# Attention scores from two full and two half-height products a tile, two tiles at a time

## The chip, the cores and the metric

The kernel runs on one core of one Trainium2 chip. The metric is the time of one execution in microseconds of device time, as a median over runs. TensorE is called PE here, VectorE DVE, ScalarE ACT, GpSimd POOL, and SyncE SP.

## The reference

`x` has the shape 4 x 1024 x 128 (batch, positions, features). Two layers follow each other, each of the form x = x + s * silu(ffn(norm(x))). The change lies in the attention of the first layer:

```python
qkv = (x @ qkv_w.T).reshape(B, S, 3, H, D)        # H = 16 heads, D = 64
q, k = rope(q), rope(k)
scores = einsum('bhqd,bhkd->bhqk', q, k) * SCALE
kb = -p * log1p(a * abs(pos_k - pos_q))           # p, a: one number a head
attn = softmax(scores + kb, axis=-1)
out = einsum('bhqk,bhkd->bhqd', attn, v)
s = out.reshape(B, S, H * D) @ out_w.T
```

There are 4 x 16 pairs of a batch and a head, each with 1024 x 1024 scores. The first layer's second part is a mixture of eight experts, the second layer a recurrence over time and a feed-forward part with low-rank additions.

## The kernel before

The program runs six blocks one after the other: `prepare`, `experts`, `project`, `attend`, `recur` and `finish`. Each block has one instruction stream for each engine, and the streams meet at semaphores. The order of the work in each stream is written out by hand.

**Numbers in two parts.** The attention works on pairs of bf16 numbers: a value is rounded to bf16 (the high part), and what the rounding left is kept as a second bf16 number (the low part). A product of two such values is put together from products of parts that are added up in PSUM.

**`project`** (lines 743 to 901) makes q and k for two heads at a time. There are 64 jobs: 8 pairs of heads, 4 batches, 2 pieces of 512 positions. In a job PE does four fp32 products of 512 columns (L900); DVE multiplies by sine and cosine and adds (L783, L784, L788) and leaves q and k of both heads in `rq`, with one head in partitions 0 to 63 and the other in 64 to 127. ACT rounds them into the high parts (`hi_part`, L796), and POOL subtracts to get the low parts (`lo_part`, L802). `parts` holds for each partition the four pieces q high, q low, k high, k low, of 512 numbers each. ACT's queue then writes all four with one DMA (`write`, L807) into the DRAM tensor `qk_parts`, whose order is (batch and pair of heads, partition, piece, position). Each of four buffers of `parts` has a semaphore `qk_wr`, which the rounding waits for before it writes the buffer again.

**Loads of scores' operands.** `load_scores_in` (L904 to L913) is called by SP for each head. It fills three tiles of 128 partitions and 1024 columns: `QS` holds q high in the upper 64 partitions and q low in the lower 64, `KS` holds k high twice and `KL` holds k low twice. Each half of a tile is one DMA of 64 rows of 2 KB, so there are six. The tiles exist twice, one set for each head of a pair.

**`attend`** (lines 923 to 1273) works on tiles of 128 queries of one head and one batch: 8 tiles are a half (`BT`), the two halves of a pair of heads are one turn of the loop (`U` = 16 tiles), and there are 32 turns (`NI`), 512 tiles in all. The turns go over the 4 batches of a pair of heads before the next pair comes. The work is a software pipeline: `step(it, u)` on each engine handles different tiles at different lags. `LV` = 2 belongs to the product with v, `LT` = 11 to the turn, `LE` = 12 to the exponent and `LS` = 13 to the scores.

- PE, `scores` (L1059): for each half of 512 keys, the product QS x KS (L1068) and QS x KL (L1069) are added in PSUM, four products of 128 rows a tile. There are two score tiles `score_ps`; before it writes one, PE waits for `biased`, which says that DVE has read the tile two before.
- DVE, `bias_max` (L1143): adds the bias table to the scores, writes them to SBUF and takes the row maximum.
- ACT, `exp` (L1224): exponents and row sums. POOL, `low` (L1256): low part of the exponents.
- PE, `turn` (L1077): eight transposes of 128 columns of the high part into `turn_ps`. ACT (L1231) or DVE (L1158) copies them out, four tiles of a half each. The low part is transposed by a DMA that SP issues (L1016).
- PE, `by_v`: in steps 0 to 3 of a half four products of 128 rows and 512 columns with the high parts (L1096), in steps 4 and 5 eight products that use 64 columns of the array each, in pairs, with the low parts (L1101).
- In step 6 DVE and ACT take the result out in two parts (`take_out`, L1163, L1166, L1236); in step 7 PE multiplies it by the output weights (`out`, 24 products of 128 columns, L1113 to L1115). DVE scales and POOL adds the shares (L1175, L1185, L1264).

In each of its steps PE does: scores, turn, `out` if it is due, `by_v` if it is due. DVE does: `take_out` if due, `bias_max`, `add_share` or `invert` if due, `scale_share` if due, copy of a turned tile if it is DVE's.

SP's stream (`units`, L1018) issues for each tile the transposing DMA, once a half the load of v, after the tiles in `LOADS` the loads for the next turn's scores, and at the tiles in `PIECES` a quarter of the bias table of the next pair of heads (only around the last batch of a pair).

Of the kernel before, what the change touches and what calls it, by code (L numbers as in the profile page):

```python
# [20 lines left out]
P = 128  # L21
# [721 lines left out]
def project(nc, K, io, sb, ps, sem):  # L743
# [46 lines left out]
    def hi_part(act, gi, j):  # L790

        s = j % 4
        act.wait_ge(pair, gi * NJ + (j + 3))

        act.wait_ge(qk_wr[s], gi * (DMA * NJ // 4) + (DMA * (j // 4) + 1))
        act.copy(parts[s][:, 0::2, :], rq[s][:]).then_inc(hi_ready, 1)  # L796

    def lo_part(g, gi, j):

        s = j % 4  # L800
        g.wait_ge(hi_ready, gi * NJ + (j + 1))
        g.tensor_tensor(parts[s][:, 1::2, :], rq[s][:], parts[s][:, 0::2, :], ALU.subtract).then_inc(lo_ready, 1)  # L802

    def write(act, gi, j):
        b, c, s = j // NC, j % NC, j % 4
        act.wait_ge(lo_ready, gi * NJ + (j + 2 + LEAD))
        act.dma_start(K.qkscr[bass.ds(gi + b * G, 1), :, :, c * CH:c * CH + CH].rearrange("o p k c -> (o p) k c"),  # L807
                      parts[s][:]).then_inc(qk_wr[s], DMA)

    with nc.Block() as block:  # L810

        @block.sync
        def _(sp):
            with sp.Fori(0, G // 2 - 1) as gh:
                for r in range(2):

                    sp.wait_ge(qk_ready, gh * (2 * NJ) + (r + 1) * NJ)
                    sp.dma_start(wqk[r][:], io["wqk"][bass.ds(gh * 2 + (r + 2), 1)].rearrange("o p k m -> (o p) k m")).then_inc(wqk_in[r], DMA)

            for s in range(4):  # L820
                sp.wait_ge(qk_wr[s], DMA * NJ // 4 + 1)

            for s in range(2):
                load_scores_in(sp, K, 0, s)
                for k in range(4):
                    load_table(sp, K, 0, s, k)
# [77 lines left out]
def load_scores_in(sp, K, ix, s):  # L904

    q = K.qkscr[bass.ds(ix % B * G + ix // B, 1)].rearrange("o p k c -> (o p) k c")
    rows = slice(s * DH, s * DH + DH)
    sp.dma_start(K.QS[s][0:DH, :], q[rows, 0, :]).then_inc(K.qk_in[s], DMA)
    sp.dma_start(K.QS[s][DH:P, :], q[rows, 1, :]).then_inc(K.qk_in[s], DMA)
    sp.dma_start(K.KS[s][0:DH, :], q[rows, 2, :]).then_inc(K.qk_in[s], DMA)  # L910
    sp.dma_start(K.KS[s][DH:P, :], q[rows, 2, :]).then_inc(K.qk_in[s], DMA)
    sp.dma_start(K.KL[s][0:DH, :], q[rows, 3, :]).then_inc(K.qk_in[s], DMA)
    sp.dma_start(K.KL[s][DH:P, :], q[rows, 3, :]).then_inc(K.qk_in[s], DMA)  # L913

# [8 lines left out]
def attend(nc, K, io, sb, ps, sem):  # L923
# [18 lines left out]
    WB, ident16 = K.WB, K.ident16  # L942
    QS, KS, KL, TB = K.QS, K.KS, K.KL, K.TB
    VV = [sb(f"v_hi_lo{s}", [P, BT, 2 * DH], BF16) for s in range(2)]
# [31 lines left out]
    LV = 2  # L976
    LS, LE, LT = LV + 11, LV + 10, LV + 9
    HI_STEPS, V_STEPS, OUT_STEP, PROJ_STEP = 4, 6, 6, 7
# [15 lines left out]
    with nc.Block() as block:  # L994

        LOADS = (BT, U - 1)
        PIECES = {BT - 2: [(0, 0)], BT - 1: [(0, 1)], BT + 1: [(0, 2)], BT + 2: [(0, 3)],
                  U - 2: [(1, 0)], U - 1: [(1, 1)], 0: [(1, 2)], 1: [(1, 3)]}

        @block.sync  # L1000
        def _(sp):
# [40 lines left out]
            for s in range(4):  # L1042
                sp.wait_ge(K.qk_wr[s], G * (DMA * S * B // CH // 4) + 1)
            for b in range(B):
# [12 lines left out]
        @block.tensor  # L1057
        def _(pe):
            def scores(it, n):  # L1059
                s, t, k = n // BT % 2, n % BT, n // U  # L1060
                if t == 0:
                    pe.wait_ge(qk_in[s], at(it, 6 * DMA, 6 * DMA * (k + 1)))
                if not (isinstance(it, int) and it == 0 and n < 2):
                    pe.wait_ge(biased, at(it, U, n - 1))
                o, q = sp_[n % 2], slice(t * P, t * P + P)
                cs = [slice(c * CH, c * CH + CH) for c in range(2)]
                for c in range(2):
                    pe.matmul(o[:, cs[c]], QS[s][:, q], KS[s][:, cs[c]], start=True, stop=False)  # L1068
                    mm = pe.matmul(o[:, cs[c]], QS[s][:, q], KL[s][:, cs[c]], start=False, stop=True)  # L1069
                mm.then_inc(s_ready, 1)  # L1070

# [46 lines left out]
            def step(it, u, there):  # L1118
                n = u + LV
                if there(u + LS):  # L1120
                    scores(it, u + LS)
                if there(u + LT):
                    turn(it, u + LT)
                if there(n) and n % BT == PROJ_STEP:
                    out(it, n // BT)
# [567 lines left out]
def program(nc, io):  # L1693

    with ExitStack() as outer:
# [18 lines left out]
        K.vscr = nc.dram_tensor("v_parts", [NT, P, H, 2 * DH], BF16, kind="Internal").ap()  # L1714
        K.qkscr = nc.dram_tensor("qk_parts", [B * G, P, 4, S], BF16, kind="Internal").ap()

# [9 lines left out]
        with ExitStack() as heads:  # L1726
            sb_in, _ = maker(heads)
            home = [K.X[:, 4 * i:4 * i + 4, :].rearrange("p t d -> p (t d)").bitcast(BF16) for i in range(6)]
            K.QS, K.KS, K.KL = [home[2 * i:2 * i + 2] for i in range(3)]
            K.TB = [sb_in(f"bias_tab{s}", [P, TAB]) for s in range(2)]  # L1730
# [79 lines left out]
```

## Time and profile before

| What | Value |
|---|---|
| median of 3 runs | 1956.33 us |
| lowest, highest | 1954.63, 1957.67 us |
| the profiled execution's own time | 1963.61 us |
| its span | 1961.8 us |
| mean granted clock of PE | 0.97 of full speed |
| PE busy | 1816.5 us |
| DVE busy | 1505.1 us |
| POOL busy | 1406.9 us |
| ACT busy | 1151.3 us |
| the queue that carries SP's and ACT's transfers | 682272 packets, 245.23 MB |
| DMA transfers of `qk_parts` into the score operands | 384 of 128 KB |

The span runs from the first to the last instruction on the core. The profiled execution took 1.8 us more than its span and 7.3 us more than the median of the runs. An engine's busy time is the sum of the stretches in which it worked. The duration of a PE product in a record contains its way through the array, so that consecutive products overlap in the records; the distance from one start to the next is what a product costs in a row of products. In a timeline, one row can stand for several instructions of the same group (x8), and its start is that of the first.

### The profile page before, as it was taken

To read this page: it belongs to the slowest core of one execution; us is meant where nothing else is said; L and a number is where in the kernel's file an instruction comes from. 1 tells how busy PE (TensorE), PEld (TensorE's weight loads), DVE (VectorE), ACT (ScalarE), POOL (GpSimd) and SP (SyncE) were. 2 spreads that over 40 slices of the span, in tenths; PEclk is the share of its full clock that TensorE was granted. 3 is DMA by queue.
4 is the path that set the end of the run, shared out by engine and by line. 5 is a ranking of instruction groups with operands and counts; after the bars stand their busy time and mean duration, and the time that the engine had idled before them with its cause. 6 is when DMAs were issued, how large, how long until landed. Compare 5 with 4: busy or idle time off the path is not lost. (4 is left out here: it accounts for less than half of the span.)

```text
span 1961.8 us, 40038 instructions
## 1 busy us (share of the span) xinstructions
PE 1816.5 (93%) x12356; PEld 1042.4 (53%) x12356; DVE 1505.1 (77%) x3016; ACT 1151.3 (59%) x1727; POOL 1406.9 (72%) x811
## 2 busy tenths in 40 slices
PE   4959989999799999999999999999999999799888
PEld 2625653333355555555555555555555555356656
DVE  5224559999788889789888888888788888688841
ACT  5525332222577777677777777777777777412133
POOL 5260217888699899799899899799899899555421
PEclk8979989999899999999999999999999999889989
DMA  4233515556488988988988988988988988500001
GB/s 153 87 106 150 159 40 168 160 169 217 148 169 189 205 184 178 191 185 179 199 187 180 192 188 181 189 187 182 188 185 181 206 189 174 129 0 1 1 6 38
DMA packets 721637, 295.28 MB, mean 151 GB/s; under 512 B 620096, under 2 KB 687682, under 8 KB 721552
## 3 DMA queue, kind: packets, MB, share of 16 engines
q1 hardware_dynamic: 682272, 245.23, 58.0%
q10 hardware_dynamic: 37248, 46.14, 6.6%
q0 software_dynamic: 2048, 3.15, 0.6%
q8 instruction: 23, 0.38, 0.1%
q14 instruction: 46, 0.38, 0.1%
HBM read 102.39 MB, written 58.85 MB: 82 GB/s over the span
## 5 line engine op out<-in xcount | busy, mean ns | idle before, releaser
L1256 POOL TENSOR_TENSOR probs_lo<-probs 128x1024 bf16<-128x1024 f32 x512 | 959.0, 1893 | 125.1 <-ACT probs L1224 68.9
L1143 DVE CUSTOM_DVE_ANT_0 scores<-score_ps,bias_tab 128x1024 f32<-128x1024 f32 x512 | 620.9, 1221 | 119.8 <-issue 117.5
L1224 ACT ACTIVATE probs<-scores,neg_max 128x1024 f32<-128x1024 f32 x512 | 587.6, 1148 | 192.7 <-DVE neg_max L1143 191.6
L1068 PE MATMUL score_ps<-x 128*128 128x512 bf16 x1024 | 391.5, 382 | 23.2 <-DVE neg_max L1143 12.0
L1069 PE MATMUL score_ps<-x 128*128 128x512 bf16 x1024 | 389.9, 381 | 0.0
L1077 PEld LDWEIGHTS turn_ps<-ident_bf,probs 128*128 128x128 bf16 x4096 | 266.7, 98 | 145.6 <-ACT probs L1224 34.3
L1077 PE MATMUL turn_ps<-ident_bf,probs 128*128 128x128 bf16 x4096 | 313.7, 220 | 9.7 <-ACT probs L1224 7.3
L1096 PE MATMUL pv_ps<-probs_t_hi,v_hi_lo 128*128 128x512 bf16 x1024 | 262.7, 379 | 0.3 <-DVE share L1175 0.3
L1231 ACT COPY probs_t_hi<-turn_ps 128x1024 bf16<-128x1024 bf16 x256 | 254.9, 996 | 2.9
L900 PE MATMUL proj_ps<-xn_t,wqk 128*128 128x512 f32 x512 | 232.7, 608 | 7.9 <-DVE rotated L788 4.0
L802 POOL TENSOR_TENSOR qk_parts<-rotated,qk_parts 128x1024 bf16<-128x1024 f32 x64 | 136.1, 2127 | 110.1 <-ACT qk_parts L796 108.8
L1068 PEld LDWEIGHTS score_ps<-x 128*128 128x128 bf16 x1024 | 100.1, 98 | 170.4 <-DVE neg_max L1143 52.3
L1158 DVE COPY probs_t_hi<-turn_ps 128x1024 bf16<-128x1024 bf16 x256 | 172.8, 675 | 0.1
L796 ACT CAST qk_parts<-rotated 128x1024 bf16<-128x1024 f32 x64 | 66.9, 1045 | 179.6 <-DVE rotated L788 143.2
L900 PEld LDWEIGHTS proj_ps<-xn_t,wqk 128*128 128x128 f32 x512 | 92.7, 191 | 147.3 <-issue 103.6
L1069 PEld LDWEIGHTS score_ps<-x 128*128 128x128 bf16 x1024 | 100.6, 98 | 91.2 <-issue 1.4
L1101 PE MATMUL pv_ps<-probs_t_lo,v_hi_lo 128*64 128x512 bf16 x1024 | 134.7, 385 | 0.0
L1460 POOL TENSOR_TENSOR q_state<-state,q_t 128x1024 f32<-128x1024 f32 x32 | 76.1, 2379 | 78.8 <-DVE state L1406 71.6
L1096 PEld LDWEIGHTS pv_ps<-probs_t_hi,v_hi_lo 128*128 128x128 bf16 x1024 | 87.1, 98 | 62.7 <-issue 0.4
L1224 ACT ACTIVATION_READ_ACCUMULATOR probs<-scores,neg_max 128x1 f32 x512 | 96.6, 189 | 0.0
L1113 PE MATMUL pv_ps<-wo_parts,out_t_hi 128*128 (+1 forms) x512 | 91.2, 221 | 2.3 <-DVE out_t_lo L1166 2.3
L1114 PE MATMUL pv_ps<-wo_parts,out_t_hi 128*128 (+1 forms) x512 | 90.5, 221 | 0.0
(228 smaller groups left out, 2404.6 us busy)
## 6 DMA issues: line engine op xcount, KB each, us to landing
x<-qk_parts SPq DMA_DIRECT2D x384, 128.0 KB, 2.9
qk_parts<-qk_parts ACTq DMA_DIRECT2D x64, 512.0 KB
v_hi_lo<-v_parts SPq DMA_DIRECT2D x64, 256.0 KB, 3.2
bias_tab<-bias_by_distance SPq DMA_DIRECT2D x64, 240.0 KB, 3.6
probs_t_lo<-probs_lo SPq DMA_TRANSPOSE x512, 3.3
v_parts<-cos_tables ACTq DMA_DIRECT2D x12, 512.0 KB
v_parts<-sin_tables ACTq DMA_DIRECT2D x12, 512.0 KB
xn<-in_x SPq DMA_DIRECT2D x4, 512.0 KB, 5.7
```

What stands on the lines that cost most here:

```text
L802: g.tensor_tensor(parts[s][:, 1::2, :], rq[s][:], parts[s][:, 0::2, :], ALU.subtract).then_inc(lo_ready, 1)
L900: mm = pe.matmul(pp[s][:, i, :], wqk[r][:, i, :], rows, start=True, stop=True)
L1068: pe.matmul(o[:, cs[c]], QS[s][:, q], KS[s][:, cs[c]], start=True, stop=False)
L1069: mm = pe.matmul(o[:, cs[c]], QS[s][:, q], KL[s][:, cs[c]], start=False, stop=True)
L1077: mm = pe.transpose(tp[n % 2][:, k, :], PRB[n % NP][:, k * P:k * P + P], ident16[:])
L1096: mm = pe.matmul(ov[i][:], VV[h][:, k, :], PT[:, r:r + 4, k, :], start=(k == 0), stop=False, skip_group_check=True)
L1101: mm = pe.matmul(ov[c][c * DH:c * DH + DH], VV[h][:, k, 0:DH], LO[:, r:r + 4, k, :], start=False, stop=(k == BT - 1), skip_group_check=True)
L1143: v.tensor_tensor_reduce(SB[n % 2][:], sp_[n % 2][:], TB[s][:, j:j + S], -1.0, 3.0e38, ALU.add, ALU.min, neg_max[:, n % 16:n % 16 + 1]).th ...
L1158: v.tensor_copy(PT[:, n % U, :, :], tp[n % 2][:]).then_inc(hi_dve, 1)
L1224: act.activation(PR[n % NP][:], SB[n % 2][:], ACT.Exp, bias=neg_max[:, m:m + 1], scale=-1.0, accum_out=row_sum[:, m:m + 1]).then_inc(exped, 1)
L1231: act.copy(PT[:, n % U, :, :], tp[n % 2][:]).then_inc(hi_act, 1)
L1256: g.tensor_tensor(LQ[n % NL][:], PR[n % NP][:], PRB[n % NP], ALU.subtract).then_inc(low_made, 1)
```

## The change

Three things change.

**The parts.** `parts` now holds q low, q high, k high, k low in this order. `qk_parts` in DRAM is ordered by (batch and pair of heads, head, piece, row of the head, position). A job is written by two DMAs of 64 partitions each, so the counts of `qk_wr` double.

**The loads.** With this order three loads of 128 rows of 2 KB fill a head's tiles: `QB` has q low above q high, `QK` has q high above k high, `KK` has k high above k low. `LOADS` moves from tiles 8 and 15 to tiles 6 and 14, and four entries of `PIECES` move forward by one tile.

**The scores.** For each half of 512 keys, a full product QB x KK gives q low x k high + q high x k low, and a product of 64 rows adds q high x k high. That product takes partitions 0 to 63 of QK and KK for the first 512 keys, and partitions 64 to 127 of QB and QK for the second 512. The product of the two low parts, which the kernel before added, is left out. In every second step PE does the full products of a tile, a turn, the full products of the next tile, and then the four half-height products of both tiles (`high_parts`); in the other steps it does a turn alone. `LS` becomes 14 and `LE` 13.

```diff
--- before.py
+++ after.py
@@ -792,20 +792,21 @@
         s = j % 4
         act.wait_ge(pair, gi * NJ + (j + 3))
 
-        act.wait_ge(qk_wr[s], gi * (DMA * NJ // 4) + (DMA * (j // 4) + 1))
-        act.copy(parts[s][:, 0::2, :], rq[s][:]).then_inc(hi_ready, 1)
+        act.wait_ge(qk_wr[s], gi * (2 * DMA * NJ // 4) + (2 * DMA * (j // 4) + 1))
+        act.copy(parts[s][:, 1:3, :], rq[s][:]).then_inc(hi_ready, 1)
 
     def lo_part(g, gi, j):
 
         s = j % 4
         g.wait_ge(hi_ready, gi * NJ + (j + 1))
-        g.tensor_tensor(parts[s][:, 1::2, :], rq[s][:], parts[s][:, 0::2, :], ALU.subtract).then_inc(lo_ready, 1)
+        g.tensor_tensor(parts[s][:, 0::3, :], rq[s][:], parts[s][:, 1:3, :], ALU.subtract).then_inc(lo_ready, 1)
 
     def write(act, gi, j):
         b, c, s = j // NC, j % NC, j % 4
         act.wait_ge(lo_ready, gi * NJ + (j + 2 + LEAD))
-        act.dma_start(K.qkscr[bass.ds(gi + b * G, 1), :, :, c * CH:c * CH + CH].rearrange("o p k c -> (o p) k c"),
-                      parts[s][:]).then_inc(qk_wr[s], DMA)
+        for h in range(2):
+            rows = K.qkscr[bass.ds(gi + b * G, 1), h, :, :, c * CH:c * CH + CH].rearrange("o k p c -> (o p) k c")
+            act.dma_start(rows, parts[s][h * DH:h * DH + DH]).then_inc(qk_wr[s], DMA)
 
     with nc.Block() as block:
 
@@ -818,7 +819,7 @@
                     sp.dma_start(wqk[r][:], io["wqk"][bass.ds(gh * 2 + (r + 2), 1)].rearrange("o p k m -> (o p) k m")).then_inc(wqk_in[r], DMA)
 
             for s in range(4):
-                sp.wait_ge(qk_wr[s], DMA * NJ // 4 + 1)
+                sp.wait_ge(qk_wr[s], 2 * DMA * NJ // 4 + 1)
 
             for s in range(2):
                 load_scores_in(sp, K, 0, s)
@@ -903,14 +904,9 @@
 
 def load_scores_in(sp, K, ix, s):
 
-    q = K.qkscr[bass.ds(ix % B * G + ix // B, 1)].rearrange("o p k c -> (o p) k c")
-    rows = slice(s * DH, s * DH + DH)
-    sp.dma_start(K.QS[s][0:DH, :], q[rows, 0, :]).then_inc(K.qk_in[s], DMA)
-    sp.dma_start(K.QS[s][DH:P, :], q[rows, 1, :]).then_inc(K.qk_in[s], DMA)
-    sp.dma_start(K.KS[s][0:DH, :], q[rows, 2, :]).then_inc(K.qk_in[s], DMA)
-    sp.dma_start(K.KS[s][DH:P, :], q[rows, 2, :]).then_inc(K.qk_in[s], DMA)
-    sp.dma_start(K.KL[s][0:DH, :], q[rows, 3, :]).then_inc(K.qk_in[s], DMA)
-    sp.dma_start(K.KL[s][DH:P, :], q[rows, 3, :]).then_inc(K.qk_in[s], DMA)
+    rows = K.qkscr[bass.ds(ix % B * G + ix // B, 1), s].rearrange("o k p c -> (o k p) c")
+    for i, dst in enumerate((K.QB, K.QK, K.KK)):
+        sp.dma_start(dst[s], rows[i * DH:i * DH + P, :]).then_inc(K.qk_in[s], DMA)
 
 
 def load_table(sp, K, g, s, k):
@@ -940,7 +936,7 @@
     recip = sem("recip")
 
     WB, ident16 = K.WB, K.ident16
-    QS, KS, KL, TB = K.QS, K.KS, K.KL, K.TB
+    QB, QK, KK, TB = K.QB, K.QK, K.KK, K.TB
     VV = [sb(f"v_hi_lo{s}", [P, BT, 2 * DH], BF16) for s in range(2)]
     SB = [sb(f"scores{i}", [P, S]) for i in range(2)]
     NP, NL = 4, 4
@@ -974,7 +970,7 @@
     NI = B * G
     U = 2 * BT
     LV = 2
-    LS, LE, LT = LV + 11, LV + 10, LV + 9
+    LS, LE, LT = LV + 12, LV + 11, LV + 9
     HI_STEPS, V_STEPS, OUT_STEP, PROJ_STEP = 4, 6, 6, 7
 
     def run(eng, step):
@@ -993,9 +989,9 @@
 
     with nc.Block() as block:
 
-        LOADS = (BT, U - 1)
-        PIECES = {BT - 2: [(0, 0)], BT - 1: [(0, 1)], BT + 1: [(0, 2)], BT + 2: [(0, 3)],
-                  U - 2: [(1, 0)], U - 1: [(1, 1)], 0: [(1, 2)], 1: [(1, 3)]}
+        LOADS = (BT - 2, U - 2)
+        PIECES = {BT - 3: [(0, 0)], BT - 1: [(0, 1)], BT: [(0, 2)], BT + 1: [(0, 3)],
+                  U - 3: [(1, 0)], U - 1: [(1, 1)], 0: [(1, 2)], 1: [(1, 3)]}
 
         @block.sync
         def _(sp):
@@ -1040,7 +1036,7 @@
             for s in range(2):
                 load_v(0, s)
             for s in range(4):
-                sp.wait_ge(K.qk_wr[s], G * (DMA * S * B // CH // 4) + 1)
+                sp.wait_ge(K.qk_wr[s], G * (2 * DMA * S * B // CH // 4) + 1)
             for b in range(B):
                 units(0, b)
             with sp.Fori(1, G - 1) as g:
@@ -1056,18 +1052,26 @@
 
         @block.tensor
         def _(pe):
+            halves = [slice(c * CH, c * CH + CH) for c in range(2)]
+
             def scores(it, n):
-                s, t, k = n // BT % 2, n % BT, n // U
-                if t == 0:
-                    pe.wait_ge(qk_in[s], at(it, 6 * DMA, 6 * DMA * (k + 1)))
+                s, k = n // BT % 2, n // U
+                if n % BT == 0:
+                    pe.wait_ge(qk_in[s], at(it, 3 * DMA, 3 * DMA * (k + 1)))
                 if not (isinstance(it, int) and it == 0 and n < 2):
                     pe.wait_ge(biased, at(it, U, n - 1))
-                o, q = sp_[n % 2], slice(t * P, t * P + P)
-                cs = [slice(c * CH, c * CH + CH) for c in range(2)]
-                for c in range(2):
-                    pe.matmul(o[:, cs[c]], QS[s][:, q], KS[s][:, cs[c]], start=True, stop=False)
-                    mm = pe.matmul(o[:, cs[c]], QS[s][:, q], KL[s][:, cs[c]], start=False, stop=True)
-                mm.then_inc(s_ready, 1)
+                q = slice(n % BT * P, n % BT * P + P)
+                for cs in halves:
+                    pe.matmul(sp_[n % 2][:, cs], QB[s][:, q], KK[s][:, cs], start=True, stop=False)
+
+            def high_parts(n):
+                s = n // BT % 2
+                for i in range(2):
+                    q = slice((n + i) % BT * P, (n + i) % BT * P + P)
+                    for c, cs in enumerate(halves):
+                        rows = slice(c * DH, c * DH + DH)
+                        mm = pe.matmul(sp_[i][:, cs], (QK, QB)[c][s][rows, q], (KK, QK)[c][s][rows, cs], start=False, stop=True)
+                    mm.then_inc(s_ready, 1)
 
             def turn(it, n):
                 pe.wait_ge(exped, at(it, U, n + 1))
@@ -1117,10 +1121,14 @@
 
             def step(it, u, there):
                 n = u + LV
-                if there(u + LS):
+                pair = there(u + LS) and (u + LS) % 2 == 0
+                if pair:
                     scores(it, u + LS)
                 if there(u + LT):
                     turn(it, u + LT)
+                if pair:
+                    scores(it, u + LS + 1)
+                    high_parts(u + LS)
                 if there(n) and n % BT == PROJ_STEP:
                     out(it, n // BT)
                 if there(n) and n % BT < V_STEPS:
@@ -1712,7 +1720,7 @@
         K.eout = nc.dram_tensor("expert_rows", [E * CAP, D], F32, kind="Internal").ap()
         K.fscr = nc.dram_tensor("bias_by_distance", [H, FLEN], F32, kind="Internal").ap()
         K.vscr = nc.dram_tensor("v_parts", [NT, P, H, 2 * DH], BF16, kind="Internal").ap()
-        K.qkscr = nc.dram_tensor("qk_parts", [B * G, P, 4, S], BF16, kind="Internal").ap()
+        K.qkscr = nc.dram_tensor("qk_parts", [B * G, 2, 4, DH, S], BF16, kind="Internal").ap()
 
         def run(block):
             with ExitStack() as own:
@@ -1726,7 +1734,7 @@
         with ExitStack() as heads:
             sb_in, _ = maker(heads)
             home = [K.X[:, 4 * i:4 * i + 4, :].rearrange("p t d -> p (t d)").bitcast(BF16) for i in range(6)]
-            K.QS, K.KS, K.KL = [home[2 * i:2 * i + 2] for i in range(3)]
+            K.QB, K.QK, K.KK = [home[2 * i:2 * i + 2] for i in range(3)]
             K.TB = [sb_in(f"bias_tab{s}", [P, TAB]) for s in range(2)]
             K.WB, K.ident16 = sb_in("wo_parts", [P, 2, H, P], BF16), sb_in("ident_bf16", [P, P], BF16)
             with ExitStack() as layer0:
```

## Rows read from the trace of the kernel before

**Rows 1.** The page, busy us, share of the span and count of instructions.

```profile
PE 1816.5 (93%) x12356; PEld 1042.4 (53%) x12356; DVE 1505.1 (77%) x3016; ACT 1151.3 (59%) x1727; POOL 1406.9 (72%) x811
```

**Rows 2.** Busy time by stretch: its length, engines' busy us, PEclk, DMA share, GB/s.

```profile
core 0: us, PE busy (x) PEld busy (x) DVE busy (x) ACT busy (x) POOL busy (x), PEclk, DMA share, GB/s
...
526.00:1686.00 1160.00, 1135.85 (x9698) 658.44 (x9698) 992.04 (x2360) 878.80 (x1344) 1034.38 (x575) 1.00 0.89 185
```

**Rows 3.** Busy time by stretch, two halves without and two with table loads.

```profile
1046.17:1081.39 35.22, 35.12 (x305) 20.56 (x304) 31.09 (x75) 27.41 (x43) 32.34 (x19) 1.00 0.85 179
1081.39:1121.12 39.73, 37.39 (x318) 21.40 (x317) 31.09 (x75) 28.26 (x44) 30.79 (x18) 1.00 0.92 192
```

**Rows 4.** The timeline of PE: start us, duration us, line, operation, tiles, count.

```profile
1013.15 0.22 PE L1113 MATMUL pv_ps<-wo_parts,out_t_hi 128*128 x1
...
1014.49 0.38 PE L1068 MATMUL score_ps<-x 128*128 128x512 bf16 x1
...
1016.67 0.38 PE L1068 MATMUL score_ps<-x 128*128 128x512 bf16 x1
...
1017.53 0.61 PE L1077 MATMUL turn_ps<-ident_bf,probs 128*128 128x128 bf16 x8
1017.98 1.03 PE L1096 MATMUL pv_ps<-probs_t_hi,v_hi_lo 128*128 128x512 bf16 x4
1018.84 0.38 PE L1068 MATMUL score_ps<-x 128*128 128x512 bf16 x1
...
1024.05 0.61 PE L1077 MATMUL turn_ps<-ident_bf,probs 128*128 128x128 bf16 x8
1024.59 1.05 PE L1101 MATMUL pv_ps<-probs_t_lo,v_hi_lo 128*64 128x512 bf16 x8
1025.58 0.39 PE L1068 MATMUL score_ps<-x 128*128 128x512 bf16 x1
```

**Rows 5.** The timeline of POOL: adding a share, then five low parts.

```profile
1019.23 1.27 POOL L1264 TENSOR_TENSOR s<-s,share 128x512 f32 x1
1020.46 9.30 POOL L1256 TENSOR_TENSOR probs_lo<-probs 128x1024 bf16<-128x1024 f32 x5
```

**Rows 6.** The timeline of DVE, around taking the result out.

```profile
1010.96 0.68 DVE L1163 CAST out_t_hi<-pv_ps 128x512 bf16<-128x512 f32 x1
1011.55 1.28 DVE L1166 TENSOR_TENSOR out_t_lo<-pv_ps,out_t_hi 128x512 bf16<-128x512 f32 x2
1012.76 1.22 DVE L1143 CUSTOM_DVE_ANT_0 scores<-score_ps,bias_tab 128x1024 f32<-128x1024 f32 x1
...
1013.91 1.22 DVE L1143 CUSTOM_DVE_ANT_0 scores<-score_ps,bias_tab 128x1024 f32<-128x1024 f32 x1
...
1028.11 0.69 DVE L1158 COPY probs_t_hi<-turn_ps 128x1024 bf16<-128x1024 bf16 x1
1028.71 0.68 DVE L1163 CAST out_t_hi<-pv_ps 128x512 bf16<-128x512 f32 x1
```

**Rows 7.** The timeline of all engines: from scores to bias pass to next scores.

```profile
1006.38 0.38 PE L1069 MATMUL score_ps<-x 128*128 128x512 bf16 x1
...
1006.81 1.22 DVE L1143 CUSTOM_DVE_ANT_0 scores<-score_ps,bias_tab 128x1024 f32<-128x1024 f32 x1 [0.95 <-issue]
...
1008.12 0.10 PEld L1068 LDWEIGHTS score_ps<-x 128*128 128x128 bf16 x1 [0.41 <-DVE neg_max L1143]
```

**Rows 8.** SP: issues in the page (count, KB, us to landing), one in the timeline.

```profile
x<-qk_parts SPq DMA_DIRECT2D x384, 128.0 KB, 2.9
...
1031.36 0.50 SPq L908 DMA_DIRECT2D x<-qk_parts  x1
```

**Rows 9.** `project`: waits of ACT (us, times, longest); the store's issue on ACT, min/median/max ns.

```profile
ACT qk_parts L796 <- DVE rotated L788: 143.2, 51, 17.5
...
L807 ACTq DMA_DIRECT2D qk_parts<-qk_parts x64: 542/549/687, 293.9 to 522.6; - x64
```

## The prediction

> **What bounds the kernel now.** I read the busy table first [rows 1]: PE is busy for 93% of the span, more than DVE or POOL. Then the busy time by stretch [rows 2]: from 526 to 1686 us, the stage `attend`, PE is busy for 1135.85 of 1160 us, with the granted clock at 1.00 (the level of 2.4 GHz). The DMA engines are busy for 0.89 of it. Scores are needed for 64 half-heads (a head and a batch, 8 tiles of 128 queries), so one half takes some 18 us. Two undisturbed halves take 35.22 us, 17.61 each; two halves in which the bias tables are reloaded take 39.73 us [rows 3].
>
> The PE timeline [rows 4] shows what fills 17.61 us. A tile's four score products take 0.86 (1016.67 to 1017.53), a turn of eight transposes 0.45, four products `by_v` on the high parts 0.86; the next scores follow at once. That is 2.17 for a step. In the two steps of each half that use the low parts, the time from turn to next scores is 1.53 instead of 1.31. The step without `by_v` takes 1.31, and the one with `out` 1.31 + 1.34 = 2.65. The sum, 4 x 2.17 + 2 x 2.39 + 1.31 + 2.65 = 17.42, is the whole half but for a small wait. So PE bounds the undisturbed halves, and score products are 6.9 us of each.
>
> The others are not far off. POOL makes five low parts in 9.30 us, 1.86 each [rows 5]: 8 x 1.86 + 1.27 = 16.15 a half. DVE is busy for 31.09 of 35.22 us [rows 3], 15.5 a half.
>
> **The products.** Eight full products a pair of tiles become four full and four with 64 rows. In the pair of halves of one tile, one product uses partitions 0 to 63 and the other 64 to 127, and they write different 512 columns of the score tile. No row shows two such products beside each other. The nearest is L1101, whose products use 64 columns of the array in pairs: eight take from 1024.59 to 1025.58, 0.99 with the way in and out, where eight after each other would take 8 x 0.215 = 1.72 [rows 4]. So pairs of half-width products run together, and I take the same for half-height ones: 0.22 a pair, 0.43 for four. The bound above is 0.86 for four, after each other; a bound below 0.43 is excluded, because each pair still streams 512 columns.
>
> **The switch.** L1101 also has a price beside its streaming: 1.53 less 1.31 is 0.22 us a step, of which 0.09 lie before it (turn at 1024.05, plus 0.45, against 1024.59) and 0.13 behind it. I take 0.22 for each group of four half-height products. The bounds are 0, if this split is free, and 0.33: a drain of what a full product's record lasts beyond its pitch (0.38 less 0.215) once on either side [rows 4]. The page TensorEngine Tiling of the Trainium skill (Key Properties) says that a change of tiling mode, not of tile, drains the engine; this speaks against the change, since four groups a half add such changes, and the 0.22 us of the L1101 rows agrees with it. It gives no time for the drain.
>
> **PE alone.** 17.42 less 4 groups x (0.86 - 0.43) = 15.70, plus 4 x 0.22 = 16.58; where a group is followed by L1101, one way out and one way in are shared, so 16.45.
>
> **The loop with DVE.** Both score tiles now fill together, so DVE finds two at once and then waits for two. Order in a pair: full products of n, turn, full products of n+1 (which wait for DVE to have read the pair before's second tile), the halves of both, `by_v`, turn, `by_v`. The pitch of the bias pass is 1.15 (1012.76 to 1013.91), of a copy 0.60, of `take_out` 0.59 + 1.21 [rows 6]; scores reach DVE 0.43 after the last product's start (1006.38 to 1006.81), 0.2 after its streaming, and the result reaches PE 1.30 after the pass began (1006.81 to 1008.12) [rows 7]. The tight place is `take_out`. From the start of DVE's pass over tile 0 of a half: pass 1.15, copy 0.60, pass 1.15, copy 0.60, `take_out` 1.80, pass 1.15, and 1.30 until the next is seen: 7.75. PE then runs from the second full products of the pair for tiles 4 and 5 to the halves of tile 0 of the next: 0.43 + 0.65 (halves and switch) + 0.86 + 0.45 + 0.86 = 3.25; the pair of tiles 6 and 7, 0.43 + 0.45 + 0.43 + 0.65 + 2.17 = 4.13; then 0.43 + 0.45 + 0.43 + 0.09 + 0.22 + 0.20 = 1.82: 9.20. Together **16.95**, half a us above PE alone. PE waits once a half, ahead of full products in the step with `by_v`'s first part; DVE waits before tiles 0 and 4. POOL's 16.15 stays under it. Exponents come in time: the turn lags the scores by three tiles instead of two at even steps, and that covers the little wait for ACT seen today.
>
> **Sum.** 17.61 - 16.95 = 0.66 a half. In halves with table loads the DMA engines set the pace: two undisturbed halves hold 0.85 x 35.22 = 29.9 us of DMA work, two with tables 0.92 x 39.73 = 36.6 [rows 3]. The bytes don't change, so I expect nothing there: 7 reloads x 2 halves. That leaves 50 x 0.66 = **33 us** (64 x 0.66 = 42 if these gain too).
>
> **The loads.** Six issues on SP of 128 KB each become three of 256 KB, at 0.50 each [rows 8]; the same 768 KB. SP spends 1.5 us a half less ahead of the transposes of low parts. It doesn't bound, so this is 0, bought by the slack that POOL has for its buffers of low parts. The loads are issued two tiles earlier for head 0 and one for head 1, while scores run one tile further ahead: some seven tiles remain, over 14 us. Table pieces move by one tile at most: 0. The start gains 1.5 us for three fewer issues, and loses some 1 to 3 as the first DVE pass waits for both tiles: 0, within 3 us.
>
> **The stores.** In `project` each job issues two DMAs of 64 rows instead of one of 128, from ACT's queue: 64 x 0.55 = 35 us more there. ACT waits there 143.2 us for DVE in all [rows 9], 2.2 a job, and DVE's three passes set the pace; both DMAs lie in that wait: 0. Without that cover it would be 35 us. High and low parts are written to other strides of the same size: 0.
>
> The profiled execution took 1963.6 (span 1961.8 and 1.8 around it), 7.3 above the median of 1956.3. So 1963.6 - 33 = 1930.6 profiled and a median of 1956.3 - 33, about **1923**.
>
> **Rivals.**
> - *The switch is free.* The loop holds 0.53 of it (three ways in, two out): 16.42 a half, 1.19 less than now, 50 x 1.19 = 60 us, a median of 1897. For it: the halves differ from full products in rows only. Against: L1101. 0.17.
> - *The drain is dearer*, 0.33 a group: five switches of 0.165 are 0.83 in the loop, 17.25 a half, 18 us gained, 1938. 0.12.
> - *The halves don't run together, and still switch.* This is the slower case: four take 0.86, a group 1.08. PE alone is 16.45 + 4 x 0.43 = 18.17 a half, 0.56 above 17.61, at 50 halves +28 us: 1984. It decides from a group cost of some 0.93 us on. For it: no such pair is in the trace, each product writes all 128 rows of its tile, and the weights of each must be loaded. Against: L1101's pairs. With other waits of that sign 0.15. The page TensorE: Matmul & The Clock Gate of the Trainium skill (Part 3, measured speedup) reports 3.07 times for four products of 32 rows; as an estimate from it, a pair of 64 would gain under the full two times and over one and a half, and a group of halves cost 0.43 to 0.57 before any switch. No row here shows it.
> - *They don't run together and don't switch* (the rows simply stay idle): eight products a pair as before, and the change doesn't do what it says. 17.4 a half, at most 5 to 10 us gained: 1950. 0.07, the case of no change.
> - *DMA becomes the bound.* 29.9 us of work in 2 x 16.95 is 0.88 instead of 0.85; today the tables bring it to 0.92 and the pace falls. If low parts come late, POOL waits and some 10 us are left: 1946. 0.06.
>
> **The numbers.** Forecast 0.43, the rivals as given; the measurement can tell 0.2% (4 us) from nothing. Faster: 0.43 + 0.17 + 0.12 + 0.06 = 0.78; same 0.07; slower 0.15. The forecast's own range is 1905 to 1935. For 8 in 10 I go down to the free switch with its few us of scatter, 1886, and up past dear drain and DMA to 1955. What is left out is the slower case, some of the case of no change, and a little below.
>
> **What would show it.** Right: two undisturbed halves take 33.9 us; four half-height products start within some 0.65 us of the start of the next group; each half has one wait of PE of about 0.5 for DVE's result ahead of full products; DVE waits longest before the pass over tile 0; ACT's stores are 128 and `project` is as long as before. A pitch of 0.215 between all halves would show the slower case; a pitch of a half to the next product equal to a full one's, the free switch. POOL waiting for DMA in undisturbed halves would show the last rival. The prediction is wrong if two undisturbed halves take over 34.9 or under 32.9 us.

## The result, and the profile after

The changed kernel takes 1913.5 us (median of 4 runs, 1911.06 to 1916.03), the kernel before 1957.0 us beside it. The ratio is 0.9775, with a 95% interval of 0.9752 to 0.9798: 43.5 us less, where 33 were forecast (1923, inside 1886 to 1955). The profiled execution took 1912.3, with a span of 1910.5.

The page of the changed kernel: busy times, and the DMA issues (count, KB each, us to landing).

```profile
PE 1750.1 (92%) x12198; PEld 951.3 (50%) x12356; DVE 1498.6 (78%) x3016; ACT 1148.3 (60%) x1727; POOL 1403.0 (73%) x811
...
x<-qk_parts SPq DMA_DIRECT2D x192, 256.0 KB, 3.4
qk_parts<-qk_parts ACTq DMA_DIRECT2D x128, 256.0 KB
```

By the page PE's busy time fell by 66 us [rows 1], but records of L1065 are missing (866 of 1024 are there), so part of that fall, and some gaps before single products, aren't real. The loads are half as many and twice as large [rows 8]. Busy time by stretch: two undisturbed halves, and two with table loads.

```profile
1008.73:1043.10 34.37, 33.47 (x300) 17.87 (x304) 30.80 (x75) 27.36 (x43) 32.20 (x19) 1.00 0.86 183
938.36:974.36 36.00, 34.05 (x300) 17.84 (x304) 30.86 (x75) 27.31 (x43) 31.34 (x18) 1.00 0.95 199
```

Against [rows 3] the undisturbed pair went from 35.22 to 34.37 us, a pair with table loads from 39.73 to 36.00. (The two pairs with table loads don't begin at the same place in the turn, so they hold different numbers of table pieces.) So the gain has two sources, and the second is one that I had put at nothing. I read a half's length from one `take_out` on DVE to the next, and call the sum of what halves take beyond the usual length of their place in the pair the surplus (61 halves of a trace). Before: 17.46 and 17.76 in turn, surplus 28.7 us. After: 16.98 and 17.39 in turn, surplus 6.7. Between the first and the last `take_out` the stage went from 1127.67 (559.20 to 1686.87) to 1078.27 (559.37 to 1637.64): 49.4 us in these two traces, 61 x 0.425 = 26 of them in usual lengths and 22 in surplus; the rest lies in the last two, shorter halves. That is 6 more than the medians show; executions of one kernel differ by such amounts.

The timeline of PE in the changed kernel, around a group of half-height products.

```profile
1008.96 0.61 PE L1073 MATMUL score_ps<-x 64*128 64x512 bf16 x4
1009.50 0.62 PE L1081 MATMUL turn_ps<-ident_bf,probs 128*128 128x128 bf16 x8
...
1017.11 0.59 PE L1065 MATMUL score_ps<-x 128*128 128x512 bf16 x2
1017.64 0.61 PE L1073 MATMUL score_ps<-x 64*128 64x512 bf16 x4
```

Four half-height products take 0.54 us to the next instruction (1008.96 to 1009.50), and the two full ones before them 0.53 (1017.11 to 1017.64) instead of 0.43. So a group costs 0.43 and 0.10 on either side: 0.63 or 0.64, where I took 0.65.

### The profile page after: what moved, and what is told of

Read it like the earlier page. It is cut to its first block and busy times, and to the rows that moved or that the text cites. A ratio compares the mean times of both kernels' runs of the same rounds, so it can differ in the third digit from the quotient of the medians.

```text
span 1910.5 us, 39672 instructions
## 1 busy us (share of the span) xinstructions
PE 1750.1 (92%) x12198; PEld 951.3 (50%) x12356; DVE 1498.6 (78%) x3016; ACT 1148.3 (60%) x1727; POOL 1403.0 (73%) x811
## 5 line engine op out<-in xcount | busy, mean ns | idle before, releaser
L1081 PEld LDWEIGHTS turn_ps<-ident_bf,probs 128*128 128x128 bf16 x4096 | 261.2, 98 | 146.7 <-issue 57.0
L1065 PE MATMUL score_ps<-x 128*128 128x512 bf16 x866 | 273.6, 383 | 44.0 <-DVE neg_max L1151 18.6
L1073 PE MATMUL score_ps<-x 64*128 64x512 bf16 x1024 | 155.9, 383 | 0.0
L1065 PEld LDWEIGHTS score_ps<-x 128*128 128x128 bf16 x1024 | 74.7, 98 | 111.9 <-DVE neg_max L1151 42.9
L783 DVE TENSOR_TENSOR proj_ps<-proj_ps,sin_tables 128x1024 f32<-128x1024 f32 x64 | 78.6, 1228 | 15.1 <-PE proj_ps L901 14.8
```

The source lines that it names most:

```text
L1065: pe.matmul(sp_[n % 2][:, cs], QB[s][:, q], KK[s][:, cs], start=True, stop=False)
L1073: mm = pe.matmul(sp_[i][:, cs], (QK, QB)[c][s][rows, q], (KK, QK)[c][s][rows, cs], start=False, stop=True)
L1081: mm = pe.transpose(tp[n % 2][:, k, :], PRB[n % NP][:, k * P:k * P + P], ident16[:])
```

## The experiments

Each kernel ran for three rounds beside the kernel before on the same chip; ratios are of medians to that kernel. Chips differ: the kernel before took 1956.4 us beside e1 to e4, 1932.7 beside e5 to e8, and 1960.4 beside the last four runs. So only ratios and half lengths are compared from one of these groups to another, and a difference of two times from different groups is a rough figure.

| Run | us | Ratio (95% interval) | Halves in turn, us | Surplus, us |
|---|---|---|---|---|
| changed kernel | 1913.5 | 0.9775 (0.9752 to 0.9798) | 16.98, 17.39 | 6.7 |
| e1_same_rows | 1973.0 | 1.0087 (1.006 to 1.0115) | 18.04, 18.49 | 0.1 |
| e2_pairs_alone | 1960.3 | 1.0023 (1.0008 to 1.0038) | 17.52, 17.83 | 26.0 |
| e3_six_loads | 1934.2 | 0.989 (0.9863 to 0.9917) | 16.98, 17.40 | 33.6 |
| e4_old_places | 1917.2 | 0.9801 (0.9772 to 0.9831) | 16.98, 17.40 | 12.0 |
| e5_new_places_before | 1924.5 | 0.996 (0.9937 to 0.9984) | 17.46, 17.76 | 24.8 |
| e6_copy_4_for_6 | 1886.5 | 0.9743 (0.9708 to 0.9777) | 17.01, 17.31 | 8.5 |
| e7_before_no_tables | 1896.9 | 0.9817 (0.979 to 0.9845) | 17.45, 17.46 | 0.0 |
| e8_after_no_tables | 1870.2 | 0.9668 (0.9639 to 0.9697) | 16.98, 17.09 | 0.0 |
| r_changed_again | 1914.8 | 0.9772 (0.9744 to 0.9801) | 16.98, 17.40 | 8.6 |
| e10_small_issues | 1928.5 | 0.9842 (0.9811 to 0.9873) | 16.98, 17.40 | 21.7 |
| e12_table_wait_first | 1906.0 | 0.973 (0.9703 to 0.9758) | 16.98, 17.09 | 10.6 |
| e13_three_together | 1888.3 | 0.9635 (0.9609 to 0.9662) | 16.50, 16.62 | 16.5 |

### Do the half-height products share the array?

```diff
-                        rows = slice(c * DH, c * DH + DH)
-                        mm = pe.matmul(sp_[i][:, cs], (QK, QB)[c][s][rows, q], (KK, QK)[c][s][rows, cs], ...)
+                        rows = slice(0, DH)
+                        mm = pe.matmul(sp_[i][:, cs], QK[s][rows, q], KK[s][rows, cs], ...)
```

> The changed kernel, but both half-height products of a tile use partitions 0 to 63 (q high and k high lie there for all 1024 keys), so the same four products of 64 rows and 512 columns a pair of tiles can't share the array. Theory (two halves of different rows run together): their pitch goes from 0.11 to 0.215 us, a group of four from 0.54 to some 0.97, PE alone needs 18.2 us a half-head, the time is some 1970 to 1985 us. Rival (a product of 64 rows is cheap by itself, or the gain comes from elsewhere): pitch and time stay, 1910 to 1918 us.

The timeline of PE of this kernel:

```profile
1003.82 1.03 PE L1073 MATMUL score_ps<-x 64*128 64x512 bf16 x4
1004.78 0.62 PE L1081 MATMUL turn_ps<-ident_bf,probs 128*128 128x128 bf16 x8
```

The same four products take 0.96 us instead of 0.54 when all use partitions 0 to 63. The time is 1973.0 and the ratio above 1, so the sharing is the whole of the change's worth in undisturbed halves. This is also what my slower rival would have given: 18.27 a half, where I had worked out 18.17. The surplus is gone here: at this pace the table loads disturb nothing.

### The order of work alone

The kernel before, with `scores` doing only the QS x KS products, `second_products` doing QS x KL for both tiles, and `LS` and `LE` one larger:

```diff
-                if there(u + LS):
+                pair = there(u + LS) and (u + LS) % 2 == 0
+                if pair:
                     scores(it, u + LS)
                 if there(u + LT):
                     turn(it, u + LT)
+                if pair:
+                    scores(it, u + LS + 1)
+                    second_products(u + LS)
```

> The kernel before with the order of work of the changed one alone: two tiles scored in one step, first the QS x KS products of both with a turn between, then the QS x KL products of both, all eight of 128 rows; stores, loads and their places as before. Theory (the gain in undisturbed half-heads is the halved products): PE alone needs 17.4 us as before and the loop with DVE 17.5, so 17.5 to 17.8 a half-head, 1950 to 1970 us, no gain. Rival (the order or the longer lead of scores brings the gain): 1940 us or less.

17.52 and 17.83 a half, ratio 1.0023: the order brings nothing by itself and costs 0.06 a half. It fits the time when all eight products are full.

### What shortened the stretches with table loads?

In e3 each of the three loads is issued in two pieces:

```diff
-        sp.dma_start(dst[s], rows[i * DH:i * DH + P, :]).then_inc(K.qk_in[s], DMA)
+        for h in range(2):
+            sp.dma_start(dst[s][h * DH:h * DH + DH, :],
+                         rows[i * DH + h * DH:i * DH + h * DH + DH, :]).then_inc(K.qk_in[s], DMA)
```

> The changed kernel with each of the three loads of 128 rows a head issued as two of 64 rows, six issues on SP as before, same bytes. Prediction's reading (the DMA engines set the pace around the table loads, SP's issues are worth nothing): 1910 to 1918 us. Rival (SP's queue is what delays the transposes of low parts around the table loads, and three issues fewer shorten that): 1922 to 1935 us, with the surplus in the half-heads with table loads.

In e4, `LOADS` and `PIECES` of the kernel before stand in the changed kernel; in e5 it is the other way round.

> The changed kernel with the places of the score loads and of the table pieces in SP's stream as before (loads after tiles 8 and 15, pieces after 6, 7, 9, 10, 14, 15, 0, 1). Prediction's reading (places are worth nothing): 1910 to 1918 us. Rival (the place after tile 15, right before the jump back of SP's loop, is what costs at each change of head pair): 1920 to 1935 us, with the surplus in the half-heads with table loads alone.

> The kernel before with only the places of the score loads and table pieces in SP's stream as in the changed kernel (loads after tiles 6 and 14, six of 64 rows each). If places matter by themselves: up to 10 us gained, 1946 to 1952 us. If only the number of issues matters: 1953 to 1960 us. In the changed kernel the new places were worth some 4 us at most (1917.2 with the old ones against 1913.5).

e10 leaves the three loads and adds three issues a head that move almost nothing:

```diff
         sp.dma_start(dst[s], rows[i * DH:i * DH + P, :]).then_inc(K.qk_in[s], DMA)
+        sp.dma_start(K.spare[0:16, s * 3 + i, :], rows[i * DH:i * DH + 16, 0:4]).then_inc(K.qk_in[s], DMA)
```

> The changed kernel with three more DMAs a head beside its three loads, each of 16 rows of 8 bytes into a tile that nobody reads: SP issues six again, the bytes and rows of the loads stay those of three. If SP's time for an issue is what six loads cost: about 20 us more than the changed kernel on the same chip, like six loads of 64 rows. If the DMA engines' work for 64 rows is what costs: within 5 us of the changed kernel.

Six loads raise the surplus from 6.7 to 33.6 us and the time by some 21 us (20.7 by the medians, 22 by the ratios), with the same bytes and unchanged undisturbed halves. Three more issues of 128 bytes each raise the surplus from 8.6 to 21.7 us and the time by 13.7 us (1928.5 against 1914.8 on the same chip). A half's loads, up to the next transpose, take SP some 1.5 us in the changed kernel, 2.9 in e10 and 3.9 in e3, so e10 adds 1.4 us of SP's time and e3 2.4: the time lost goes about in step with it, though e10 moves next to no bytes. So most of the price, and as far as these runs show all of it, is SP's time for issuing. That e3's 64-row transfers also cost the DMA engines something isn't ruled out.

Old places cost 3.7 us by the medians and some 5 by the surplus; the two intervals overlap, so that size stays unsure. New places alone give the kernel before a ratio of 0.996, some 8 us, of which its surplus shows 4.

A measure of SP's room is how long it waits for POOL's low parts, from the waits of SP's queue (us in total, times, longest) of the kernel before, of the changed kernel, of e3 and of e10. They are taken from 540 us to 1687 for the kernel before and to 1640 for the others, which leaves out the last 14 to 22 us of `attend` in e10 and e3:

```profile
SPq L1015 <- POOL probs_lo L1256: 57.9, 122, 1.5
```

```profile
SPq L1011 <- POOL probs_lo L1264: 141.9, 226, 2.0
```

```profile
SPq L1012 <- POOL probs_lo L1265: 31.9, 77, 0.9
```

```profile
SPq L1012 <- POOL probs_lo L1265: 82.1, 162, 1.5
```

Of some 1100 us SP waited 57.9 for POOL before, so its queue was some 95% full, and I hadn't read that view. From the changed kernel to e10 and e3 the surplus rises as that room falls: 6.7 us at 141.9, 21.7 at 82.1, 33.6 at 31.9. It is a rough measure: e4 has the changed kernel's room (142.4) and a surplus of 12.0, and e7, with 59.6, has none, because without table loads nothing piles up. Who pays can be seen in POOL's waits for the transposing DMAs, before and after (in e10 they are 34.2 us, in e3 61.0):

```profile
POOL probs_lo L1256 <- DMA probs_t_lo<-probs_lo: 47.3, 40, 3.6
```

```profile
POOL probs_lo L1264 <- DMA probs_t_lo<-probs_lo: 13.8, 18, 2.3
```

A late transpose keeps a buffer of low parts, and POOL stops. Six issues of 64 rows take SP 3.75 us in a half of e3, three of 128 rows 1.38 in the changed kernel. The six of the kernel before took as long as e3's, 3.74 from 1031.36 [rows 8] to the end of the last. The timelines of SP of e3, of the changed kernel and of the kernel before:

```profile
1016.13 3.75 SPq L910 DMA_DIRECT2D x<-qk_parts  x6
```

```profile
1007.91 1.38 SPq L909 DMA_DIRECT2D x<-qk_parts  x3
```

```profile
1034.55 0.55 SPq L913 DMA_DIRECT2D x<-qk_parts  x1
```

The traces show one more thing about where the surplus lies. In SP's stream the stage is a loop with one pass for each middle pair of heads, and at each of its five jumps back SP issues nothing for 3.5 to 4.7 us, in the kernel before and in the changed one. The timeline of SP in the changed kernel, around one of them:

```profile
941.67 0.45 SPq L916 DMA_DIRECT2D bias_tab<-bias_by_distance  x1
946.36 1.27 SPq L1012 DMA_TRANSPOSE probs_t_lo<-probs_lo  x1
```

All of the changed kernel's surplus lies in the five halves that hold such a jump, and so do 17 us of the 28.7 before and 28.6 of e3's 33.6. The gap alone costs nothing: e7 and e1 have it too, of 3.4 us and more, without a surplus. It costs where SP is already late with table pieces and loads. What SP does in it the traces don't say, and no run took the loop away, so its share isn't shown.

### The tables themselves

In e7 (on the kernel before) and e8 (on the changed one) no tables are reloaded, and all heads use those of the first pair. DVE's wait for a table then has a constant value.

```diff
-                    for s, k in PIECES.get(n, ()):
+                    for s, k in ():
...
-                    v.wait_ge(tab_in[s], (it + n // U) // B * (4 * DMA) + 4 * DMA)
+                    v.wait_ge(tab_in[s], 4 * DMA)
```

> The kernel before without the reloads of the bias tables: all heads use the tables of the first pair, 56 DMAs of 240 KB are left out. The surplus of the half-heads with table loads over 17.61 adds up to some 29 us in the trace of before, so 1925 to 1932 us.

> The changed kernel without the reloads of the bias tables (all heads use the first pair's). Its trace shows a surplus of some 6 us in those half-heads, so 1905 to 1909 us. If the tables cost both kernels the same, about 1885 us.

The kernel before gains 35.8 us, more than its surplus of 29. On the changed one the ratio falls from 0.9772 to 0.9668, some 20 us of 1932.7 and more than its surplus of 7 to 9. The expected times were worked out for the chips of the earlier runs, so only the gains can be held against them: 29 and 6 expected, and both missed. What comes on top in both is that the longer half of each pair got shorter: 17.76 to 17.45, and 17.39 to 17.09. That pointed to the wait's value. The line of that wait in the changed kernel shows its arithmetic, once a turn of 16 tiles (min/median/max ns):

```profile
L1146 DVEq FUSED_REGOPS  x31: 112/115/115, 555.6 to 1593.4; - x31
```

e12 does nothing but put this wait ahead of the one for the scores:

```diff
-                v.wait_ge(s_ready, at(it, U, n + 1))
                 if t == 0:
                     v.wait_ge(tab_in[s], (it + n // U) // B * (4 * DMA) + 4 * DMA)
+                v.wait_ge(s_ready, at(it, U, n + 1))
```

> The changed kernel with DVE's wait for the bias table ahead of its wait for the scores, so that the register arithmetic for that wait's value (0.11 us, once in 16 tiles) runs while DVE waits anyway. If this arithmetic makes the one half-head of a pair longer: 16.98 and 17.09 us instead of 16.98 and 17.39, some 32 x 0.3 = 9 us less than the changed kernel. Otherwise no change.

The halves are 16.98 and 17.09, and the time is 8.8 us below the changed kernel's on the same chip. The arithmetic had run after the scores were there, in DVE's stretch of the loop; now it runs while DVE waits. The timeline of the changed kernel shows the 0.30 in place: in the longer half DVE's pass over tile 0 begins 0.73 us after the group that completes its scores, in the shorter one 0.44 (the pass at 1022.21 is shown further down). In e12 it is 0.44 in both.

```profile
1004.49 0.61 PE L1073 MATMUL score_ps<-x 64*128 64x512 bf16 x4
...
1005.22 1.23 DVE L1151 CUSTOM_DVE_ANT_0 scores<-score_ps,bias_tab 128x1024 f32<-128x1024 f32 x1
...
1021.77 0.61 PE L1073 MATMUL score_ps<-x 64*128 64x512 bf16 x4
```

Of these 0.29 us the arithmetic's own record is 0.11; what the rest is isn't shown.

### Is the loop around `take_out` the bound?

```diff
-        DVE_TILES, ACT_TILES = (1, 3, 5, 6), (0, 2, 4, 7)
+        DVE_TILES, ACT_TILES = (1, 3, 4, 5), (0, 2, 6, 7)
```

(PE's wait for tile 6 ahead of `by_v` is left out as well, since tile 7, which ACT copies after it, is waited for.)

> The changed kernel with the copies of turned tiles dealt out otherwise: DVE copies tiles 1, 3, 4, 5 and ACT 0, 2, 6, 7 (before tile 6 was DVE's and tile 4 ACT's). Theory (undisturbed half-heads are set by the loop of DVE and PE around take_out): the loop loses one copy of 0.60 and PE alone, 16.45, or the loop at 16.35 plus the 0.24 measured beyond my count, is next: 16.5 to 16.8 a half-head instead of 17.19, 1880 to 1895 us. Rival (PE alone or another engine already bounds): 1908 us or more.

A miss: 17.01 and 17.31, a tenth less in the longer half and 0.03 more in the shorter. (The time, 1886.5, lies in the expected range only because this chip runs every kernel faster; the ratio, 0.9743, is 0.3% below the changed kernel's.) The timeline of DVE shows why; a new wait took the place of the copy that left:

```profile
998.88 1.22 DVE L1150 CUSTOM_DVE_ANT_0 scores<-score_ps,bias_tab 128x1024 f32<-128x1024 f32 x1
...
1000.02 0.69 DVE L1170 CAST out_t_hi<-pv_ps 128x512 bf16<-128x512 f32 x1
...
1001.12 1.29 DVE L1173 TENSOR_TENSOR out_t_lo<-pv_ps,out_t_hi 128x512 bf16<-128x512 f32 x2 [0.41 <-ACT out_t_hi L1243]
...
1002.33 1.22 DVE L1150 CUSTOM_DVE_ANT_0 scores<-score_ps,bias_tab 128x1024 f32<-128x1024 f32 x1
```

From pass to pass over `take_out` it is 3.45 us where it had been 1.15 + 0.60 + 1.80 = 3.55: ACT now copies tile 6 (999.61 to 1000.5) before it rounds its part of the result, and DVE subtracts that part first. e13 turns this order round, with e6 and e12 kept:

```diff
-                for c in range(2):
+                for c in (1, 0):
                     v.wait_ge(ot_hi[c], at(it, 2, hh + 1))
...
-                for c in range(2):
+                for c in (1, 0):
                     pe.wait_ge(ot_ready[c], at(it, 2, hh + 1))
...
-                v.wait_ge(op_ready, at(it, 4, 2 * hh + 1))
+                v.wait_ge(op_ready, at(it, 4, 2 * hh + 2))
```

> The changed kernel with DVE copying tile 4 instead of 6 as in the run before (which left 17.01 and 17.31, because DVE then waited 0.41 us for ACT's part of take_out), the table wait first, and DVE and PE taking the second half of the result first, so that ACT's part may come later. Theory (the loop of DVE and PE around take_out sets the pace, PE alone needs 16.45): 16.5 to 16.7 us a half-head, 25 to 40 us less than the changed kernel. If DVE's loop was not the bound: 16.98 stays and only the 9 us of the table wait are gained.

16.50 and 16.62 a half, ratio 0.9635 (0.9609 to 0.9662): 26.5 us below the changed kernel on the same chip, and the best version found. The undisturbed halves are now 0.05 and 0.17 us above PE's own 16.45, as worked out in the prediction. The surplus is 16.5 us, more than the changed kernel's 8.6 on that chip: at a faster pace SP's room shrinks again, to 113.1 us.

```profile
SPq L1011 <- POOL probs_lo L1263: 113.1, 205, 1.2
```

## Why the prediction was right, and where it wasn't

Two undisturbed halves took 34.37 us, where 33.9 were forecast and over 34.9 or under 32.9 would have been wrong.

**The products: right.** Pairs of half-height products run together, 0.43 for four beside the switch; e1 shows it by taking the pairing away, and e2 that the order of work alone gains nothing.

**The switch: right in size.** 0.10 on either side of a group, 0.22 taken. The free switch and the dear drain both fall, and so does the slower rival, whose 18.17 a half is what e1 measured within 0.1.

**The loop with DVE: right for one half of each pair.** These rows of the changed kernel are its timeline, of PE and of DVE: the second full products of the pair for tiles 4 and 5, DVE's pass over tile 0, its pass over tile 3, and the next such products of PE.

```profile
1012.97 0.61 PE L1065 MATMUL score_ps<-x 128*128 128x512 bf16 x2
```

```profile
1022.21 1.22 DVE L1151 CUSTOM_DVE_ANT_0 scores<-score_ps,bias_tab 128x1024 f32<-128x1024 f32 x1 [1.08 <-issue]
...
1028.66 1.22 DVE L1151 CUSTOM_DVE_ANT_0 scores<-score_ps,bias_tab 128x1024 f32<-128x1024 f32 x1
```

```profile
1030.18 0.38 PE L1065 MATMUL score_ps<-x 128*128 128x512 bf16 x1 [0.33 <-DVE neg_max L1151]
```

PE's part is 1022.21 - 1012.97 = 9.24 (9.20 worked out). DVE's is 28.66 - 22.21 = 6.45 and 1.30 until the next products begin, 7.75 (7.75). The record of the first product at 1030 is missing, as the count of 1 suggests and its weight load shows:

```profile
1029.95 0.11 PEld L1065 LDWEIGHTS score_ps<-x 128*128 128x128 bf16 x2 [0.27 <-DVE neg_max L1151]
```

That the two parts add up to the half, 16.99 to 16.98 (16.95), is so by construction; what bears the prediction out is that each part has the length worked out for it. That taking 0.6 out of it works only together with ACT's part (e6, e13) and then ends at PE's own sum supports the loop and the sum. The two were changed with e12 in one kernel, so the share of the order of `take_out` alone wasn't tried.

**Missed in the loop: 0.30 in the other half.** The prediction worked with a mean half of 17.61 and never asked why the two halves of a pair differ (17.46 and 17.76); it put what was left over its sum down to a small wait of PE for ACT. The inequality was DVE's register arithmetic between two waits (e7, e8, e12), which stays and stands in the tighter loop. So the usual half became 17.19 instead of 16.95, and 0.425 instead of 0.66 were gained on it: 26 us over 61 halves. With the arithmetic out of the way (e12) 0.11 of the inequality is left, which no run explains.

**The step that failed: the loads, "It doesn't bound, so this is 0", and with it "In halves with table loads the DMA engines set the pace".** I took the DMA share of 0.92 in [rows 3] for a bound, without reading the waits of SP's queue. But that share can go higher without any loss of pace. These are a half with table loads of the kernel before, and one of the changed kernel:

```profile
1081.39:1100.64 19.25, 18.97 (x166) 11.16 (x165) 15.61 (x38) 14.45 (x23) 16.38 (x10) 1.00 1.02 209
```

```profile
920.97:938.36 17.39, 16.91 (x154) 9.01 (x154) 15.45 (x38) 13.85 (x22) 16.45 (x10) 1.00 1.14 231
```

Both moved 4.02 MB. The changed kernel did it in 17.39 us, the half's usual length, at a share of 1.14. In e13 the share is 0.95 over all of 526 to 1610 us. What set the stretches before was SP: eight transposes, six loads, v and table pieces nearly filled its time. e3 and e10 put a price on three issues a head of some 21 and 14 us, where the prediction had 0. The saving was mis-sized too: 1.5 us of SP's time a half, from 0.50 an issue, where the time between issues counts as well and 3.75 became 1.38. This term and the half of the loop that was missed have opposite signs, so that 1923 lies near 1913.5 is partly luck: 33 forecast from undisturbed halves, against 26 in usual lengths and 22 in surplus by the traces. The page DMA: Bandwidth & Descriptors of the Trainium skill (Issuing engines are not separate DMA queues) calls the sequencer's time to start a DMA usually small beside the DMA itself. The trace agrees for a single one, 0.46 us of issue against 3.4 to landing (256 KB). Yet here it was the term that counted, since the queue was full: 0.46 us an issue of 256 KB and 0.63 of 128 KB in the rows above.

**The stores: right.** ACT issued 128 of them at a median of 625 ns, 80 us instead of 35, so 45 more where 35 were worked out, and waited 8.8 us for them (7.3 before); the stage before `attend` isn't longer, with the first `take_out` at 559.37 against 559.20.

## What to carry to other kernels

Read the waits of the issuing queue as one reads those of an engine: what it waits for is its room, and a DMA share near 0.9 doesn't say that the DMA engines bound: look for a stretch with a higher share that kept its pace. When a product is split so that half of it has half the rows, let pairs take different rows and group them, because each group pays for a switch on both sides. Before moving an instruction off an engine in a loop, look for what the receiving engine must do next for that same loop, and put a wait whose value needs arithmetic ahead of the one that comes last.

## What the runs showed of the hardware

- Two products of 64 rows and 512 columns, on partitions 0 to 63 and 64 to 127 and to different 512 columns of PSUM, take together what one full product takes: four in 0.54 us with 0.10 of switch, and 0.96 if all use the same rows.
- Entering and leaving such a group costs 0.10 us each, about what L1101, whose pairs take different columns, costs (0.09 and 0.13).
- Register arithmetic for a wait's value takes DVE 0.11 us by its record. Where it stood behind the wait that came last, the next pass began 0.29 us later, and the half was 0.30 longer.
- The share of busy DMA engines reached 1.14 in a half that kept its usual length, so it isn't a measure with its limit at 1.
- SP issued nothing for 3.5 to 4.7 us at each jump back of its loop in `attend`, in the kernel before and in the changed one.
- The kernel before took 1932.7 us on one chip and 1956.4 and 1960.4 on others. The undisturbed halves were the same (17.46 and 17.76 in e5), while the first `take_out` of e5 came at 527.51 instead of 559.20: the difference lies mostly ahead of that. Why is open.
- Not settled: the 0.11 us by which the halves of a pair still differ with e12.
